# Two Toeplitz convolutions as block-diagonal matrix products between transposes, in place of shifted multiply-adds

## The chip, the cores and the metric

The kernel runs on one core of a Trainium2 chip. The metric is device time in microseconds (us) for one launch. TensorE, VectorE, ScalarE, GpSimd and SyncE are PE, DVE, ACT, POOL and SP in the profile; PEld is PE loading a stationary matrix. Everything is in float32 unless a row says f16.

## What is computed

The input is 8 images of 16 x 16 places with 96 channels, 2048 tokens in all. Four layers follow each other: L0 (a block-wise product in the 2-D Fourier domain, then an MLP), L1 (the Toeplitz layer), and L2 and L3 (each a layer norm, four recurrent GRU passes over 256 steps, a gate and a projection). The change concerns L1:

```python
xn = srms(x)
u = jax.nn.silu(xn @ Wu + bu)
v = jax.nn.silu(xn @ Wv + bv)                # 192 channels
a_h = tno_coeffs(H, r2_...)                  # per channel, 31 lags, from a small network
a_w = tno_coeffs(W, r1_...)
out = tno_apply(v, a_h, -3) + tno_apply(v, a_w, -2)   # by FFT of length 32
return (u * out) @ Wo + bo + x
```

`tno_apply` is, for each channel by itself, a product with a 16 x 16 Toeplitz matrix along the rows (axis 0 in the kernel) or along the columns (axis 1) of the image.

## The kernel before

The order of the work is written out by hand, engine by engine, with semaphores. The program is a row of blocks; all engines meet at the end of each. The ones that matter here are the MLP (function `mlp`) and L1 (function `toeplitz`). All DMAs are issued by SP in the order written.

Two layouts alternate. In a token layout, the 128 partitions are tokens and each of 16 tiles holds 96 channels (`stream`, `rows`). In a channel layout, the partitions are the 96 channels of one of two chunks `m`, and the free dimension is the 2048 tokens, worked in 4 banks of 512 (`xT`, `u`, `v`, `acc`).

The MLP block starts with a norm (`norm_vector`: small chained operations, then 16 row scalings), 16 transposes, and two matrix products. POOL adds a bias to the residual meanwhile.

`toeplitz` does this:
1. Norm and 16 transposes (L139, L163); ACT copies the result into `xT` (L733). POOL adds the output bias to `stream` (L653).
2. 16 products with 512 columns (L766) give `v`, then `u`, in channel layout; ACT applies SiLU twice for `v` (float32 and float16) and once for `u`. POOL makes small diagonal matrices out of the coefficients (L670).
3. The lags. `PE_LAGS` names 18 of the 62 (axis, lag) pairs, done on PE for both chunks as products with float16 diagonal matrices in three parts, accumulated in PSUM (L785). The other 44 pairs are in `DVE_LAGS`: one multiply-add over the shifted image for each chunk, 88 in all, each into the same accumulator `acc` (L692).
4. After the last lag DVE adds PE's part (L714) and multiplies by `u` (L719), 8 times each; PE projects (L798) once the `gated` semaphore allows, bank by bank; DVE adds to `base` (L723) and takes the statistics for the next norm (L147).

Beside this, weights of L2 and L3 are split in a high and a low part: the high part on ACT (L842, L843), the low part on POOL after its diagonals (L848, L851).

The coefficients themselves (`coef`, 96 x 2 x 2 x 31) are ready before the MLP block begins.

## Time and profile before

| | us |
|---|---|
| median of three runs (lowest, highest) | 1206.0 (1205.65, 1208.2) |
| the profiled execution | 1204.91 |
| its span | 1203.1 |
| PE busy in the span | 1085.8 |
| DVE busy | 950.9 |
| ACT busy | 773.5 |
| POOL busy | 154.9 |
| MLP block, by the timeline | 91.2 to 127.5 |
| L1 block | 127.9 to 272.5 |
| L2 from | 272.6 |

The span is the profiler's first to last instruction. It lies 1.8 us below the profiled execution's own time. The two recurrent layers take over 900 us of it. Busy shares are means over the span and say little of one stage; the stage has to be read by windows of time.

### The profile page before, as it was taken

Reading aid. Unit: us, or ns where it says so; the run is one execution under the profiler, and the core shown is the slowest. Engines: PE = TensorE matmul, PEld = TensorE weight load, DVE = VectorE, ACT = ScalarE, POOL = GpSimd, SP = SyncE. Lnnn points to the kernel's source line nnn. Section 1 sums busy time; section 2 is a strip of 40 time slices with the busy share of each in tenths; the row PEclk is TensorE's granted clock in tenths of the full one; section 3 lists DMA queues with packets and bytes.
Section 4 is the critical chain, followed back from the end, with each engine's and each line's share of the span. In section 5 each row is a group of like instructions: output and inputs, shape, how many; then the busy total and the mean of one; then the engine's idle time right before and its main releaser. Section 6 shows DMA issues by size and latency. Waiting matters only on the chain. (4 is left out here: it accounts for less than half of the span.)

```text
span 1203.1 us, 55551 instructions
## 1 busy us (share of the span) xinstructions
PE 1085.8 (90%) x22424; PEld 860.0 (71%) x22424; DVE 950.9 (79%) x5703; ACT 773.5 (64%) x4503; POOL 154.9 (13%) x222
## 2 busy tenths in 40 slices
PE   3787799958999999999999989999999999999997
PEld 2554344445888888888888866788888888888886
DVE  3544699987888888888888876788888888888884
ACT  4223530007788788777777773788788777777773
POOL 1001379920000000001000100000000001000100
PEclk9587899957555555555555556555555555555555
DMA  4000500000000000000000000000000000000000
GB/s 121 2 1 12 133 1 1 1 0 7 4 4 4 4 4 4 4 4 4 4 4 4 3 4 5 4 4 3 4 4 4 4 3 4 4 4 4 4 4 27
DMA packets 8220, 12.59 MB, mean 10 GB/s; under 512 B 5746, under 2 KB 7122, under 8 KB 7675
## 3 DMA queue, kind: packets, MB, share of 16 engines
q1 hardware_dynamic: 7962, 9.05, 3.0%
q8 instruction: 175, 2.87, 1.0%
q14 instruction: 83, 0.67, 0.2%
HBM read 8.26 MB, written 0.79 MB: 8 GB/s over the span
## 5 line engine op out<-in xcount | busy, mean ns | idle before, releaser
L1077 DVE TENSOR_TENSOR_SCAN L3s_h_hi<-L3s_renew,L3s_terms 96x32 f16<-96x32 f32 x512 | 114.5, 224 | 64.3
L1077 DVE TENSOR_TENSOR_SCAN L2s_h_hi<-L2s_renew,L2s_terms 96x32 f16<-96x32 f32 x512 | 114.5, 224 | 64.2
L1185 PE MATMUL L3s_reset_sum<-L3s_h_hi,L_w_hidden 97*128 97x8 f16 x2048 | 139.6, 179 | 11.6 <-DVEq L1054 0.4
L1185 PE MATMUL L2s_reset_sum<-L2s_h_hi,L_w_hidden 97*128 97x8 f16 x2048 | 139.6, 179 | 11.6 <-DVEq L1054 0.4
L1112 POOL TENSOR_TENSOR L_y<-L_states 96x64 f32<-96x64 f32 x128 | 40.9, 355 | 843.1 <-DVE L_states L1079 843.1
L1185 PEld LDWEIGHTS L3s_reset_sum<-L3s_h_hi,L_w_hidden 97*128 97x128 f16 x2048 | 94.4, 107 | 62.1 <-DVE L3s_h_hi L1077 13.8
L1185 PEld LDWEIGHTS L2s_reset_sum<-L2s_h_hi,L_w_hidden 97*128 97x128 f16 x2048 | 94.4, 107 | 62.1 <-DVE L2s_h_hi L1077 13.8
L1133 ACT ACTIVATE L3s_terms<-L3s_cand 96x16 f32<-96x16 f32 x512 | 111.5, 218 | 37.5 <-DVE L3s_cand L1063 6.0
L1133 ACT ACTIVATE L2s_terms<-L2s_cand 96x16 f32<-96x16 f32 x512 | 111.5, 218 | 37.4 <-DVE L2s_cand L1063 5.9
L1185 PE MATMUL L3s_cand_sum<-L3s_h_hi,L_w_hidden 97*128 97x8 f16 x2048 | 131.3, 175 | 4.5 <-DVE L3s_h_hi L1077 3.1
L1185 PE MATMUL L2s_cand_sum<-L2s_h_hi,L_w_hidden 97*128 97x8 f16 x2048 | 131.3, 175 | 4.5 <-DVE L2s_h_hi L1077 3.1
L1185 PE MATMUL L3s_keep_sum<-L3s_h_hi,L_w_hidden 97*128 97x8 f16 x2048 | 130.0, 174 | 0.0
L1185 PE MATMUL L2s_keep_sum<-L2s_h_hi,L_w_hidden 97*128 97x8 f16 x2048 | 130.0, 174 | 0.0
L1128 ACT ACTIVATE L3s_reset<-L3s_reset_sum 96x16 f32<-96x16 f32 x512 | 93.0, 182 | 53.2 <-PE L3s_reset_sum L1185 1.1
L1128 ACT ACTIVATE L2s_reset<-L2s_reset_sum 96x16 f32<-96x16 f32 x512 | 93.0, 182 | 53.2 <-PE L2s_reset_sum L1185 1.0
L1185 PE MATMUL L3s_reset_sum<-L3s_h_lo,L_w_hidden 96*128 96x8 f16 x1024 | 114.1, 185 | 0.5 <-DVE L3s_h_lo L1085 0.2
L1185 PE MATMUL L2s_reset_sum<-L2s_h_lo,L_w_hidden 96*128 96x8 f16 x1024 | 114.0, 185 | 0.4 <-DVE L2s_h_lo L1085 0.2
L1185 PE MATMUL L3s_keep_sum<-L3s_h_lo,L_w_hidden 96*128 96x8 f16 x1024 | 112.1, 183 | 0.0
L1185 PE MATMUL L2s_keep_sum<-L2s_h_lo,L_w_hidden 96*128 96x8 f16 x1024 | 112.1, 183 | 0.0
L1063 DVE TENSOR_TENSOR_SCAN L3s_cand<-L3s_reset,L3s_cand_sum 96x32 f32<-96x32 f32 x512 | 110.4, 216 | 2.0 <-ACT L3s_reset L1128 1.1
L1063 DVE TENSOR_TENSOR_SCAN L2s_cand<-L2s_reset,L2s_cand_sum 96x32 f32<-96x32 f32 x512 | 110.4, 216 | 2.0 <-ACT L2s_reset L1128 1.1
L692 DVE SCALAR_TENSOR_TENSOR l_acc<-l_v,coef,l_acc 96x384 f32<-96x384 f32 (+11 forms) x88 | 103.6, 1241 | 0.4
(257 smaller groups left out, 3517.9 us busy)
## 6 DMA issues: line engine op xcount, KB each, us to landing
L_wih_raw<-in_L_wih SPq DMA_DIRECT2D x2, 1152.0 KB, 11.4
l_w_raw<-in_L_w SPq DMA_DIRECT2D x1, 1296.0 KB
L_w_hidden_raw<-in_L_whh SPq DMA_DIRECT2D x2, 576.0 KB
stream<-in_x SPq DMA_DIRECT2D x2, 384.0 KB, 3.8
out<-stream SPq DMA_DIRECT2D x4, 192.0 KB, 2.1
l_idft<-in_idft SPq DMA_DIRECT2D x1, 400.0 KB
rpe_lw<-in_rpe_lw SPq DMA_DIRECT2D x1, 384.0 KB
l_dft<-in_dft SPq DMA_DIRECT2D x1, 288.0 KB, 2.9
```

What stands on the lines that cost most here:

```text
L692: e.scalar_tensor_tensor(out=row(to, acc), in0=row(of, v), scalar=coef[:, m, axis, at:at + 1], in1=row(to, acc), op0=ALU.mult, op1=ALU.add ...
L1063: e.tensor_tensor_scan(flat(cand[g][:, x]), flat(reset[g][:, x]), flat(cand_sum(g, p)[0:C, :, :, s]), 0.0, ALU.mult, ALU.add).then_inc(can ...
L1077: e.tensor_tensor_scan(flat(h_hi[g][0:C, x]), flat(renew[g][:, x]), flat(terms[g][:, x]), 0.0, ALU.mult, ALU.add).then_inc(hi_ready[g], 1)
L1112: e.tensor_tensor(y[:, m, :, t:t + STEPS].rearrange("p b t -> p t b"), hist[g0][:, t:t + STEPS, j0, :], mirrored, ALU.add)
L1128: e.activation(reset[g][:, x, :, 1], reset_sum(g, p)[0:C, :, s], ACT.Sigmoid).then_inc(advanced[g], 1)
L1133: e.activation(terms[g][:, x, :, 0], cand[g][:, x, :, 1], ACT.Tanh).then_inc(advanced[g], 1)
L1185: return e.matmul(dst, weights.hidden[0:rows, wp, GATES * (2 * g + j) + gate, :], rhs, start=False, stop=False, skip_group_check=True)
```

## The change

The lags disappear from DVE and PE. In their place, for each axis, PE multiplies with matrices of 128 x 128. The 128 entries are 8 channels by 16 places, so that a Toeplitz product is one block-diagonal matrix: `lagged`, for 2 axes and 24 octets of channels.

To fill `lagged`, POOL sets it to zero at the start of the MLP block (128 x 6144 values); SP writes `coef` to a DRAM buffer, waits for that and for the zeros, and issues 16 DMAs of 16 partitions x 24 x 16 values. Each run of 16 values is 64 bytes.

`v` is now made in token layout, once for each axis: 16 tiles of 128 tokens that share one place (row or column), 192 channels each, two to a bank. ACT writes them with one place in every sixteenth element. The bias is a 97th row of `xT` that POOL sets to one. `xT` is stored by row, then image, then column. Then for axis 1 and after it axis 0:
- PE transposes 24 blocks of 128 x 128 (L783) and DVE copies them, four to a copy (L693);
- PE multiplies each with its matrix (L796) and DVE copies the result back into token layout, writing elements 192 apart (L697).

Back in channel layout, PE transposes 32 blocks for axis 1 (L806), and ACT copies them to `both` with elements 256 apart (L746); then 32 blocks for axis 0 (L815), which DVE adds (L706), and multiplies by `u` (L710). The projection waits for halves of the image rather than for quarters. The bias goes into `stream` in place, once the norm has read it.

The diff, cut to its core:

```diff
+                e.dma_start(coefs.rearrange("(m c) a l -> c m a l", m=CHUNKS), coef[:]).then_inc(coefs_written, 16)
+                e.wait_ge(coefs_written, 16)
+                e.wait_ge(cleared, 1)
+                for octet in range(8):
+                    mine = slice(octet * SIDE, (octet + 1) * SIDE)
+                    for axis in range(2):
+                        e.dma_start(lagged[mine, axis, :, mine], lagged_layout(coefs, octet, axis)).then_inc(lagged_loaded, 16)
...
+                e.memset(lagged[:], 0.0).then_inc(cleared, 1)
...
-PE_LAGS = [(axis, lag) for axis, lags in ((0, range(-5, 5)), (1, range(-4, 4))) for lag in lags]
...
+def lagged_layout(coefs, octet, axis):
+    flat_coefs = coefs.rearrange("c a l -> (c a l)")
+    return bass.AP(flat_coefs.tensor, octet * 2 * LAGS + axis * LAGS, [[1, SIDE], [8 * 2 * LAGS, OCTETS], [1, SIDE]])
...
+        xT = sb("xT", [C + 1, TOKENS])
...
+        values = [sb(f"values{axis}", [P, D1 * SIDE]) for axis in range(2)]
+        by_place = [x[:].rearrange("p (c r) -> p r c", r=SIDE) for x in values]
+        convolved = [x[:].rearrange("p (w c) -> p w c", w=SIDE) for x in values]
+        blocks = sb("blocks", [P, OCTETS, P])
+        rows = blocks[:].rearrange("p n q -> p (n q)")[:, 0:TILES * C].rearrange("p (t c) -> p t c", c=C)
+        both = sb("both", [C, CHUNKS, TOKENS])
...
+                e.memset(xT[C:C + 1, :], 1.0).then_inc(ones_ready, 1)
+                e.wait_ge(ones_ready, 1)
+                e.wait_ge(loaded, 96)
+                e.wait_ge(norm.rows_ready, TILES)
+                e.tensor_tensor(stream[:], stream[:], b_o[:].unsqueeze(1).to_broadcast([P, TILES, C]), ALU.add)\
...
-                    e.scalar_tensor_tensor(out=row(to, acc), in0=row(of, v), scalar=coef[:, m, axis, at:at + 1],
-                                           in1=row(to, acc), op0=ALU.mult, op1=ALU.add).then_inc(acc_step[m], 1)
...
+                for a, axis in enumerate(ORDER):
+                    for i in range(GROUPS_OF_4):
+                        e.wait_ge(block_done, GROUPS_OF_4 * a + i + 1)
+                        e.tensor_copy(blocks[:, 4 * i:4 * i + 4, :],
+                                      bank(BLOCKS_AT[a] + i)[:].rearrange("p (n q) -> p n q", n=4)).then_inc(block_saved, 1)
+                    for i in range(GROUPS_OF_4):
+                        e.wait_ge(conv_done, GROUPS_OF_4 * a + i + 1)
+                        e.tensor_copy(convolved[axis][:, :, 32 * i:32 * i + 32].rearrange("p w c -> p c w"),
+                                      bank(CONV_AT[a] + i)[:].rearrange("p (c w) -> p c w", w=SIDE)).then_inc(conv_saved, 1)
...
+                        n = CHUNKS * k + m
+                        mine = both[:, m].rearrange("p (b h w) -> p h b w", b=BATCH, h=SIDE)[:, 4 * k:4 * k + 4]
+                        by_row = lambda x: x.rearrange("p (h b w) -> p h b w", h=4, b=BATCH)
+                        e.wait_ge(first_saved, CHUNKS * NB)
+                        e.wait_ge(back_done, CHUNKS * NB + n + 1)
+                        e.tensor_tensor(mine, mine, by_row(bank(BACK + 8 + n)[0:C, :]), ALU.add)\
+                            .then_inc(both_added, 1)
+                        e.wait_ge(both_added, n + 1)
+                        e.wait_ge(u_ready, CHUNKS * NB)
+                        e.tensor_tensor(mine, mine, by_row(u[:, m, k * BANK:(k + 1) * BANK]), ALU.mult).then_inc(gated, 1)
...
+                    e.activation(by_row[:, 2 * k:2 * k + 2], bank(TURNED + k)[0:C, :].rearrange("p (b h w) -> p b h w", b=2, h=SIDE),
+                                 ACT.Copy).then_inc(copied, 1)
+                for a, axis in enumerate(ORDER):
+                    for i in range(V_GROUPS):
+                        n = V_GROUPS * a + i
+                        e.wait_ge(v_done, n + 1)
+                        e.activation(by_place[axis][:, SIDE - 2 - 2 * i:SIDE - 2 * i, :],
+                                     bank(VALUES + n)[:, 0:2 * D1].rearrange("p (r c) -> p r c", r=2), ACT.Silu).then_inc(v_ready, 1)
...
+                        e.wait_ge(back_done, NB * m + k + 1)
+                        e.activation(both[:, m].rearrange("p (b h w) -> p w h b", b=BATCH, h=SIDE)[:, 4 * k:4 * k + 4],
+                                     bank(BACK + NB * m + k)[0:C, :].rearrange("p (w h b) -> p w h b", w=4, h=SIDE), ACT.Copy)\
+                            .then_inc(first_saved, 1)
...
+                        for slot in range(2):
+                            place = 2 * i + 1 - slot
+                            tile = xT[:, place * P:(place + 1) * P] if axis == 0 else image[:, :, place]
+                            last = e.matmul(bank(VALUES + n)[:, slot * D1:(slot + 1) * D1], tile, w_v[:], start=True, stop=True)
...
+                        for j in range(4):
+                            octet = 4 * i + j
+                            last = e.transpose(bank(BLOCKS_AT[a] + i)[:, j * P:(j + 1) * P],
+                                               values[axis][:, octet * P:(octet + 1) * P], ident[:])
+                        last.then_inc(block_done, 1)
+                    if a == 0:
+                        e.wait_ge(lagged_loaded, 16 * 16)
+                    for i in range(GROUPS_OF_4):
+                        if i < 2 and a == 0:
+                            e.wait_ge(u_ready, 6 + i + 1)
+                        elif i < 2:
+                            e.wait_ge(conv_saved, 4 + i + 1)
+                        e.wait_ge(block_saved, GROUPS_OF_4 * a + i + 1)
+                        for j in range(4):
+                            octet = 4 * i + j
+                            last = e.matmul(bank(CONV_AT[a] + i)[:, j * P:(j + 1) * P], blocks[:, octet, :],
+                                            lagged[:, axis, octet, :], start=True, stop=True)
+                        last.then_inc(conv_done, 1)
...
+                            last = e.transpose(bank(BACK + n)[0:C, j * P:(j + 1) * P],
+                                               convolved[ORDER[0]][:, 4 * k + j, m * C:(m + 1) * C], ident[:])
...
+                        e.wait_ge(first_saved, n + 1)
+                        for j in range(4):
+                            last = e.transpose(bank(BACK + 8 + n)[0:C, j * P:(j + 1) * P],
+                                               convolved[ORDER[1]][:, 4 * k + j, m * C:(m + 1) * C], ident[:])
+                        last.then_inc(back_done, 1)
...
+                    e.wait_ge(gated, 4 * (half + 1))
```

On PE, from the end of the `u` products on, there stood before:

```order
L785 MATMUL l_bank<-l_v_hi,l_diag 128x512 [waits l1_diag_ready,l1_u_ready,l1_v_hi_ready]
L785 MATMUL l_bank<-l_v_hi,l_diag 128x512 x3
L785 MATMUL l_bank<-l_v_hi,l_diag 128x512 [waits l1_diag_ready]
L785 MATMUL l_bank<-l_v_hi,l_diag 128x512 x3
L785 MATMUL l_bank<-l_v_lo,l_diag 128x512 [waits l1_v_lo_ready,l1_diag_ready]
L785 MATMUL l_bank<-l_v_lo,l_diag 128x512 x3
L785 MATMUL l_bank<-l_v_hi,l_diag 128x2x176 [waits l1_diag_ready]
L785 MATMUL l_bank<-l_v_hi,l_diag 128x2x176 x3
```

and this went on for 432 instructions. `l_v_hi`, `l_v_lo` are the float16 parts of `v`, `l_diag` the diagonal matrices. Now there stand, at the end of the first axis's transposes and at the start of the transposes back:

```order
L783 MATMUL l_bank<-ident,l_values 128x128 [waits l1_u_ready]
L783 MATMUL l_bank<-ident,l_values 128x128 x3
L796 MATMUL l_bank<-lagged,l_blocks 128x128 [waits l1_block_saved,l1_u_ready,lagged_loaded]
L796 MATMUL l_bank<-lagged,l_blocks 128x128 x3
L796 MATMUL l_bank<-lagged,l_blocks 128x128 [waits l1_block_saved,l1_u_ready]
L796 MATMUL l_bank<-lagged,l_blocks 128x128 x3
L796 MATMUL l_bank<-lagged,l_blocks 128x128 [waits l1_block_saved]
...
L806 MATMUL l_bank<-ident,l_values 96x128 [waits l1_conv_saved]
L806 MATMUL l_bank<-ident,l_values 96x128 x23
L806 MATMUL l_bank<-ident,l_values 96x128 [waits l1_conv_saved]
```

`l_values` holds SiLU of `v` and later the convolved values, `l_blocks` the transposed blocks. Of the 432 products 48 of another kind are left, and 48 transposes before and 64 behind them are new. The first product waits for `lagged_loaded`.

On DVE, from the norm's row scalings on, there stood before:

```order
L139 TENSOR_SCALAR l_rows<-stream,l1n_rstd 128x96 [waits l1n_chained]
L139 TENSOR_SCALAR l_rows<-stream,l1n_rstd 128x96 x15
L696 MEMSET l_acc 96x2048 x2
L680 TENSOR_TENSOR l_v_lo<-l_v,l_v_hi 96x2048 [waits l1_v_hi_ready]
L692 SCALAR_TENSOR_TENSOR l_acc<-l_v,coef,l_acc 96x8x176 [waits l1_acc_step0]
L692 SCALAR_TENSOR_TENSOR l_acc<-l_v,coef,l_acc 96x8x160 [waits l1_acc_step0] x2
L692 SCALAR_TENSOR_TENSOR l_acc<-l_v,coef,l_acc 96x8x144 [waits l1_acc_step0] x2
```

followed by the rest of the 88 multiply-adds. Now the program has:

```order
L139 TENSOR_SCALAR l_blocks<-stream,l1n_rstd 128x96 [waits l1n_chained]
L139 TENSOR_SCALAR l_blocks<-stream,l1n_rstd 128x96 x15
L693 COPY l_blocks<-l_bank 128x512 [waits l1_block_done] x6
L697 COPY l_values<-l_bank 128x32x16 [waits l1_conv_done] x6
L693 COPY l_blocks<-l_bank 128x512 [waits l1_block_done] x6
L697 COPY l_values<-l_bank 128x32x16 [waits l1_conv_done] x6
L706 TENSOR_TENSOR l_both<-l_both,l_bank 96x4x8x16 [waits l1_back_done,l1_first_saved]
L710 TENSOR_TENSOR l_both<-l_both,l_u 96x4x8x16 [waits l1_u_ready,l1_both_added]
```

and the last two rows seven times more. The 88 dependent multiply-adds, two clears and two subtractions are gone; 24 copies out of PSUM stand in their place, and the additions and products with `u`, eight each as before, now alternate.

## Rows read from the trace of the kernel before

**Rows 1.** Which stages there are: PE, PEld, DVE, ACT, POOL busy, granted clock, DMA.
```profile
91.20:127.50 36.30, 28.27 (x136) 18.91 (x136) 14.24 (x58) 13.05 (x19) 3.42 (x1) 0.77 0.04 10
127.90:155.90 28.00, 19.94 (x48) 6.97 (x48) 22.14 (x47) 19.62 (x33) 9.36 (x12) 0.82 0.61 143
155.90:242.40 86.50, 83.31 (x432) 41.33 (x432) 86.47 (x74) 5.78 (x4) 83.36 (x66) 1.00 0.00 1
242.40:257.00 14.60, 0.03 (x1) 0.03 (x1) 14.29 (x17) 0.00 (x0) 6.63 (x2) 0.57 0.00 0
257.00:272.50 15.50, 13.95 (x64) 13.70 (x64) 12.11 (x32) 0.00 (x0) 0.00 (x0) 0.50 0.00 0
```

**Rows 2.** Groups by line, 140 to 400 us: count, busy, mean ns, idle.
```profile
L692 DVE SCALAR_TENSOR_TENSOR l_acc<-l_v,coef,l_acc 96x384 f32<-96x384 f32 (+11 forms) x88 | 103.6, 1241 | 0.4
```

**Rows 3.** Timeline from 92 us: start, length, engine, line, operation, count, idle.
```profile
92.43 0.17 DVE L122 TENSOR_SCALAR mlpn_power<-mlpn_moments 128x16 f32<-128x16 f32 x1
...
93.80 7.10 DVE L136 TENSOR_SCALAR l_rows<-l_spatial,mlpn_moments,mlpn_rstd 128x96 f32<-128x96 f32 x16
...
94.78 3.42 POOL L417 TENSOR_TENSOR l_residual<-l_residual,mlp_b 128x1536 f32<-128x1536 f32 x1 [35.36 <-DMA mlp_affine<-in_L_norm]
...
120.78 5.50 PE L467 MATMUL l_bank<-mlp_w,mlp_hidden 128*128 128x96 f32 x48
...
130.76 6.55 DVE L139 TENSOR_SCALAR l_rows<-stream,l1n_rstd 128x96 f32<-128x96 f32 x16
...
131.09 3.42 POOL L653 TENSOR_TENSOR l_base<-stream,l_b_o 128x1536 f32<-128x1536 f32 x1 [32.90 <-DMA l_b_o<-in_L_b_o]
...
138.81 16.34 PE L766 MATMUL l_bank<-l_xT,l_w_uv 96*96 96x512 f32 x32 [0.77 <-ACT l_xT L733]
```

**Rows 4.** Timeline around the end of the stage.
```profile
254.44 1.28 DVE L714 TENSOR_TENSOR l_acc<-l_acc,l_bank 96x512 f32<-96x512 f32 x2
...
256.98 13.97 PE L798 MATMUL l_bank<-l_w_o,l_v 96*128 96x96 f32 x64 [14.61 <-DVE l_v L719]
...
270.98 0.56 DVE L723 TENSOR_TENSOR stream<-l_base,l_bank 128x384 f32<-128x384 f32 x1 [2.09 <-PE l_bank L798]
...
275.61 3.92 DVE L136 TENSOR_SCALAR L2i_rows<-stream,L2n_moments,L2n_rstd 128x96 f32<-128x96 f32 x16
```

**Rows 5.** Groups by shape, 235 to 249 us, VectorE.
```profile
L692 DVE SCALAR_TENSOR_TENSOR l_acc<-l_v,coef,l_acc 96x640 f32<-96x640 f32 x2 | 9.8, 4904 | 0.0
L692 DVE SCALAR_TENSOR_TENSOR l_acc<-l_v,coef,l_acc 96x256 f32<-96x256 f32 x1 | 3.3, 3307 | 0.0
```

**Rows 6.** Timeline at the start of the last layer.
```profile
737.40 1.80 POOL L907 MEMSET L_forward<- 1x2048 f16 x1 [20.75 <-POOLq L1234]
...
738.67 0.56 DVE L122 TENSOR_SCALAR L3n_power<-L3n_moments 128x16 f32<-128x16 f32 x1
```

**Rows 7.** Groups by shape, first 127 us: busy, mean ns.
```profile
L389 PE MATMUL l_bank<-l_by_freq,l_idft 100*128 100x384 f32 x32 | 10.9, 497 | 0.9 <-ACT l_by_freq L336 0.9
...
L379 PE MATMUL l_bank<-ident,l_mixed 128*36 128x128 f32 x64 | 8.6, 305 | 1.4 <-ACT l_mixed L328 1.4
...
L318 ACT ACTIVATE l_spectrum<-l_bank,l_affine 96x288 f32<-96x288 f32 x8 | 4.5, 756 | 0.0
...
L247 POOL MEMSET l_by_freq<- 100x3072 f32 x1 | 2.7, 2658 | 3.0 <-POOLq L1297 3.0
...
L300 DVE COPY l_spatial<-l_bank 128x384 f32<-128x384 f32 x4 | 2.2, 558 | 7.5 <-PE l_bank L389 7.5
```

**Rows 8.** The same for 128 to 156 us.
```profile
L733 ACT ACTIVATE l_xT<-l_bank 96x512 f32<-96x512 f32 x4 | 2.4, 594 | 6.5 <-PE l_bank L163 6.5
```

**Rows 9.** Timeline of the first layer's transposes.
```profile
67.21 8.64 PE L379 MATMUL l_bank<-ident,l_mixed 128*36 128x128 f32 x64 [1.35 <-ACT l_mixed L328]
```

**Rows 10.** Granted clock (before the last two) where only transposes run, from 67.2 us.
```profile
66.00:70.00 4.00, 2.79 (x14) 2.01 (x15) 1.47 (x8) 3.31 (x10) 0.00 (x0) 0.50 0.00 0
70.00:72.00 2.00, 2.00 (x19) 1.74 (x18) 1.41 (x5) 1.11 (x4) 0.00 (x0) 0.93 0.00 0
72.00:74.00 2.00, 2.00 (x21) 1.80 (x19) 1.65 (x5) 1.48 (x5) 0.00 (x0) 1.00 0.01 4
```

**Rows 11.** The DMA queue, 127 to 131 us: packets, MB, share of 16 engines.
```profile
q1 hardware_dynamic: 492, 0.35, 41.7%
```

More of the change, by code:

```diff
@@ L390, in _, with mlp @@
                     last.then_inc(inverted, 1)
-def mlp(nc, d, stream, spatial, residual, rows, banks, ident, stats):
+def mlp(nc, d, stream, spatial, residual, rows, banks, ident, stats, coef, coefs, lagged, lagged_loaded):
     with ExitStack() as ctx:
@@ L596, in finish, with toeplitz @@
                         .to_broadcast([C, CHUNKS, 2, LAGS]), ALU.add).then_inc(self.finished, 1)
-PE_LAGS = [(axis, lag) for axis, lags in ((0, range(-5, 5)), (1, range(-4, 4))) for lag in lags]
-PE_LAGS.sort(key=lambda al: al != (0, 0))
-DVE_LAGS = [(axis, lag) for axis in range(2) for lag in sorted(range(1 - SIDE, SIDE), key=abs) if (axis, lag) not in PE_LAGS]
-def shifted(v, axis, lag):
-    n = SIDE - abs(lag)
-    to, of = (slice(lag, SIDE), slice(0, n)) if lag >= 0 else (slice(0, n), slice(-lag, SIDE))
-    return to, of
-def toeplitz(nc, d, stream, ident, coef, weights, stats):
+OCTETS = D1 // 8
+def lagged_layout(coefs, octet, axis):
+    flat_coefs = coefs.rearrange("c a l -> (c a l)")
+    return bass.AP(flat_coefs.tensor, octet * 2 * LAGS + axis * LAGS, [[1, SIDE], [8 * 2 * LAGS, OCTETS], [1, SIDE]])
+def toeplitz(nc, d, stream, ident, lagged, lagged_loaded, weights, stats):
     with ExitStack() as ctx:
@@ L639, in toeplitz, with tiles_of @@
         banks = [ctx.enter_context(nc.psum_tensor(f"l1_bank{i}", [P, BANK], F32)) for i in range(8)]
+        TURNED, VALUES, INNER, BLOCKS_AT, CONV_AT, BACK, OUT = 0, 4, 20, (28, 40), (34, 46), 52, 68
+        bank = lambda n: banks[n % 8]
+        V_GROUPS, GROUPS_OF_4 = SIDE // 2, OCTETS // 4
+        ORDER = (1, 0)
+        def tiles_of(rows, k):
+            first = 8 * (k % 2) + k // 2
+            return rows[:, first:first + 2 * 4 - 1:2, :]
         with nc.Block() as block:
@@ new lines, in _ @@
+                for a, axis in enumerate(ORDER):
[4 more added lines that the diff above has]
+                                     bank(VALUES + n)[:, 0:2 * D1].rearrange("p (r c) -> p r c", r=2), ACT.Silu).then_inc(v_ready, 1)
+                e.wait_ge(loaded, 96)
+                for m in range(CHUNKS):
+                    for k in range(NB):
+                        e.wait_ge(u_done, NB * m + k + 1)
+                        e.activation(u[:, m, k * BANK:(k + 1) * BANK], bank(INNER + NB * m + k)[0:C, :], ACT.Silu,
+                                     bias=b_u[:, m:m + 1]).then_inc(u_ready, 1)
@@ new lines, in _ @@
+                image = xT[:].rearrange("p (n w) -> p n w", w=SIDE)
+                for a, axis in enumerate(ORDER):
+                    for i in range(V_GROUPS):
+                        n = V_GROUPS * a + i
+                        if n >= 8:
+                            e.wait_ge(v_ready, n - 7)
+                        for slot in range(2):
+                            place = 2 * i + 1 - slot
+                            tile = xT[:, place * P:(place + 1) * P] if axis == 0 else image[:, :, place]
+                            last = e.matmul(bank(VALUES + n)[:, slot * D1:(slot + 1) * D1], tile, w_v[:], start=True, stop=True)
+                        last.then_inc(v_done, 1)
@@ new lines, in _ @@
+                e.wait_ge(conv_saved, 2 * GROUPS_OF_4)
+                for k in range(NB):
+                    for m in range(CHUNKS):
+                        n = CHUNKS * k + m
+                        e.wait_ge(first_saved, n + 1)
+                        for j in range(4):
+                            last = e.transpose(bank(BACK + 8 + n)[0:C, j * P:(j + 1) * P],
+                                               convolved[ORDER[1]][:, 4 * k + j, m * C:(m + 1) * C], ident[:])
+                        last.then_inc(back_done, 1)
@@ L792, in _ @@
                 for k in range(NB):
-                    e.wait_ge(gated, CHUNKS * (k + 1))
+                    half = k // 2
+                    e.wait_ge(gated, 4 * (half + 1))
                     for t in range(4):
-                        tile = 4 * k + t
+                        tile = HALVES * (4 * (k % 2) + t) + half
                         for m in range(CHUNKS):
-                            last = e.matmul(banks[k][:, t * C:(t + 1) * C], v[:, m, tile * P:(tile + 1) * P], w_o[:, m, :],
+                            last = e.matmul(bank(OUT + k)[:, t * C:(t + 1) * C], both[:, m, tile * P:(tile + 1) * P], w_o[:, m, :],
```

190 lines of the change are left out of this document (59 added, 131 removed).

## The prediction

> **What bounds the kernel now.** I read the busy time by windows first, because the shares over the whole span are nearly all recurrent layers, which the change does not touch. In the L1 block the reader should see three stretches [rows 1]. From 155.9 to 242.4 us PE, DVE and POOL are all full (83.3, 86.5 and 83.4 of 86.5 us). Then PE stops and DVE goes on alone to about 257. From 257 to 272.5 PE projects at a granted clock of 0.50, that is 1.2 GHz. Second, the groups by line: the 88 lags on DVE are 103.6 us with 0.4 us idle before them [rows 2]. They wait for nothing. Third, the timeline: DVE ends its last lag at 254.44 and the projection starts at 256.98 [rows 4], whereas PE's last lag ends at 242.4. So DVE's chain sets the end, with PE 12 us behind it. Removing DVE's lags alone would be worth 12 us; this change takes both away.
>
> **The sum** is made on the profiled execution (1204.91 us, span 1203.1); the median of the runs, 1206.0, is 1.1 above. Everything before 91.2 and behind 272.5 keeps its length.
>
> (a) *MLP block.* POOL now starts with a clear of 6144 values. One of 3072 took 2.66 [rows 7], so this one takes 5.3, from 91.2 to 96.5. A clear does hold up DVE: in the last layer POOL's ran from 737.40 to 739.20, and the TENSOR_SCALAR that started at 738.67 lasted 0.56 instead of the 0.17 it takes in the MLP [rows 3, 6], to 739.23. In the MLP this same operation starts at 92.43, the row scalings at 93.80 [rows 3]. I let it wait to 96.5. Then POOL's addition of 3.42 follows and, as before (7.10 for scalings that alone take 3.92 [rows 3, 4]), shuts DVE out, to about 100.1. The remaining small operations, then 16 scalings of 3.92, end at 104.5 instead of 100.9: **+3.6**. Bounds 0 (DVE gets in between) and 5.3.
> The DRAM round trip and the 16 DMAs run beside the MLP. They hold 6144 runs of 64 bytes. From 127 to 131 the queue took 41.7% of 16 engines for 492 packets [rows 11]: 0.417 x 16 x 4.0 / 492 = 54 ns each, so 6144 / 16 x 54 ns = 21 us, from about 98 to 119, plus issues. They are needed near 162: 0.
>
> (b) *Norm of L1.* POOL's bias addition (3.42) ran during the row scalings, which took 6.55; it now waits until they are through, and they cost 3.92: **-2.6**. It then runs beside PE and ACT only. The clear of the row of ones is 1.8 long (as the 2048-value clear [rows 6]) and over before the scalings.
>
> (c) *`v` and `u`.* Before: 138.81 to 155.9, 17.1. Now 32 products of 192 columns, two passes each. A warm pass with 384 columns is 10.93/32 = 0.342, one with 96 columns 5.50/48 = 0.115 [rows 3, 7]; these are the bounds, and I take 0.18 for 192: 64 x 0.18 = 11.5. `u` is 16 passes of 512, 0.342 x 512/384 = 0.46 each, 7.3. A slow start is 0.5. Together 19.3: **+2.2**. ACT's 16 SiLUs have 384 values each, written 64 bytes apart. The nearest row writes 288 values 32 bytes apart in 0.56 (4.5/8 [rows 7]), 1.9 ns each, against 0.594/512 = 1.2 for contiguous ones [rows 8]. That gives 0.45 to 0.75 each, 7 to 12 in all, about PE's own time. SP has six loads instead of four to issue ahead of the recurrent weights; they have 10 us until PE needs them.
>
> (d) *From the last `u` to the end of the block.* Before: 155.9 to 272.5, 116.6. Now:
> - Transposes and products, two axes. A transpose is 8.64/64 = 0.135 [rows 7, 9], so 24 are 3.2. A product of 128 columns is two passes of 0.13 (bounds 0.115 and 0.342), 24 are 6.2. Twice 9.4 is 18.8. DVE's 24 copies of 512 values are 0.74 each by the 384-value copy (0.558 [rows 7]), 17.8 in all. Most lie beside PE. The first block copies of an axis must be through before the next products, and so on: four hand-overs of 0.5, 2.0. Sum **20.8**. The writes 768 bytes apart could double half of the copies, which adds about 2.2 for each axis.
> - Back: DVE may add only when ACT has copied all 8 banks of axis 1. ACT takes 0.59 contiguous, 1.0 at the price of the strided row; I take 0.8: 6.4, and 1.0 for the first four transposes and the hand-overs: **7.4**. PE's 64 transposes (8.6) and the second set are hidden behind ACT and DVE.
> - DVE: 16 operations of 0.64 (1.28 for two [rows 4]) and waits of 0.06 are 11.2; the first half of the image is gated at 5.6. PE then projects. Before, it idled 14.6 and then ran all 13.97 at the low clock [rows 1, 4]; now it idles about 5 and I keep the low clock: 7.0 for the first half, to 12.6, 7.0 for the second, to 19.6, and 1.5 for the last addition, statistics and block end: **21.1**. At the high clock it would be 11.2 + 3.8 + 1.5 = 16.5.
> The three make 49.3 instead of 116.6: **-67.3**.
> POOL's low parts of the weights, about 13 us, run from about 164 now, beside DVE's copies. Before, they stretched DVE's lags to 3.3 and 4.9 us [rows 5], but those read two SBUF operands; the copies read PSUM. I take 0; the other end is +10.
>
> Sum: 3.6 - 2.6 + 2.2 - 67.3 = -64.1, which is 1140.8 on the profiled execution and **1142** on the median.
>
> **Two rules weighed.** The clock: in the first layer PE does only transposes from 67.21 to 75.85 [rows 9]. The granted clock is 0.50 up to 70, 0.93 from 70 to 72, then 1.00 [rows 10], so it rose while only transposes ran. The Trainium skill (TensorE: Matmul & The Clock Gate, Part 4: PE-mode transpose) says that transposes don't bring the array to its high clock. By that rule the 24-transpose stretches would drag the clock down; the trace disagrees, but with float32 and 36 columns held, so the case stays a rival; by the rule the sum would be rival 2's 1161, by the trace it is 1142.
> The strides: the only strided ACT row costs 1.6 times a contiguous one per value [rows 7, 8]. The Trainium skill (SBUF — State Buffer, Door 1: The DMA port swizzle) says that SBUF has lines of 16 bytes and that each access crossing to a new line pays. By it all new layouts (64, 768 and 1024 bytes) pay on every value; the trace agrees in direction at 32 bytes. The sum by the rule would be rival 1's.
>
> **The rivals.**
> 1. *Strided accesses cost double* (13%). For: the 1.9 ns row. Against: `v` is only 384 values per operation. Price: 16 SiLUs at 1.5 instead of 0.75 add 12 beyond PE's 11.5, DVE's strided copies 2 x 2.2, ACT's copies back 8 x 0.4: about 19. Time 1161.
> 2. *PE stays at the low clock in (d)* (14%). For: its bursts are short and wait on copies; the projection before ran 14 us busy at 0.50 and did not rise. Against: [rows 10], and `v`, `u` are dense. Price: 18.8 doubled, as all its passes are column-bound: +18.8. Time 1161.
> 3. *Better than the sum* (11%): the clear does not hold DVE (-3.6), the projection runs warm (-4.6), ACT's copies are contiguous-priced (-1.6). Time 1132.
> 4. *POOL blocks DVE's copies too* (5%): +10, 1152.
> 5. *Slower than before* (3%): the 16 loads touch only 16 partitions each. If their runs are spread over few DMA engines, they take 6144 x 54 ns = 332 us on one, from 98 to 430, and the first product, due at about 163, waits 267 us: 1142 + 267 = 1409. It loses from a load that ends 64 us late, at 227, thus below 332/129 = 2.6 engines. Nothing in the trace shows a DMA to 16 partitions. Against it: the 54 ns come from loads of 96 and 128 partitions that kept 41.7% of 16 engines busy.
> That the lags are not really gone is excluded by the order of the instructions.
>
> **How the numbers follow.** The forecast has 54%, with its own range 1133 to 1152. With rivals 1 to 4 the range is 1128 to 1165; outside lie the DMA case, both clock and strides together, and the best cases. A measurement here can tell 0.2%, 2.4 us, from no change. All but rival 5 are faster by far more: faster 0.96, same 0.01, slower 0.03.
>
> **What would show it.** In the changed profile: the MLP's first TENSOR_SCALAR lasting to about 96.5; L1's scalings in 3.9; `v` passes of 0.17 to 0.19 and SiLUs of at most 0.75; 20 us for the transposes and products at a clock of 1.00; ACT's strided copies under 1.0; the projection in two bursts of 7; PE waiting nowhere on `lagged`; L2 starting near 208. It is wrong if PE waits for the loads, if copies out of PSUM last 3 us beside POOL, or if the two recurrent layers change their length.

## The result, and the profile after

The changed kernel takes **1134.96 us** (median of 4 runs, 1133.43 to 1139.38); the kernel before, run beside it, 1205.83 (4 runs). The ratio is **0.9418**, 95% interval 0.9386 to 0.945: faster by 71 us. Run again beside the kernels of experiments 3 and 5, the same kernel took 1137.03 (5 runs, 1133.87 to 1140.01), ratio 0.9444 (0.9423 to 0.9465). Forecast: 1142, range 1128 to 1165.

In the profiled execution (1135.26 us, span 1133.1) the stages stand so:

| stage | before | after | change | forecast |
|---|---|---|---|---|
| up to the MLP block | 91.1 | 92.3 | +1.2 | 0 |
| MLP block | 36.75 | 37.3 | +0.5 | +3.6 |
| L1 to the first `v` product | 10.9 | 7.6 | -3.3 | -2.6 |
| `v` and `u` | 17.2 | 19.2 | +2.1 | +2.2 |
| from the last `u` to L2 | 116.6 | 45.9 | -70.7 | -67.3 |
| L2 to the end | 930.5 | 930.7 | +0.2 | 0 |
| sum | | | -70.0 | -64.1 |

The 1.2 us ahead of the MLP block need not come from the change. In `no_dve_lags` and `one_pe_lag` (experiment 4), which are the kernel before up to L1, this block starts at 92.5 and 92.6 too.

The windows of the changed kernel by stage (length, busy time of PE, PEld, DVE, ACT, POOL with counts, granted clock, DMA share, GB/s) answer to [rows 1]:

```profile
91.20:127.50 36.30, 24.82 (x134) 17.52 (x134) 17.02 (x54) 13.05 (x19) 8.61 (x2) 0.81 0.17 22
129.60:156.50 26.90, 22.92 (x97) 18.03 (x98) 5.25 (x39) 21.89 (x31) 5.24 (x2) 0.87 0.66 149
156.50:173.50 17.00, 16.12 (x146) 15.94 (x144) 16.39 (x23) 6.50 (x5) 12.51 (x4) 1.00 0.00 1
173.50:186.80 13.30, 7.86 (x65) 6.75 (x65) 6.98 (x11) 7.18 (x8) 0.00 (x0) 0.92 0.00 0
186.80:200.80 14.00, 13.95 (x64) 13.71 (x64) 8.88 (x24) 0.00 (x0) 0.00 (x0) 0.50 0.01 1
```

The 86.5 us with three full engines and the 14.6 us of DVE alone are gone. In their place stand 17.0 us in which PE and DVE are both nearly full (16.12 and 16.39 busy), at a granted clock of 1.00; PE sets the pace, for it waits only once. Then follow 13 us in which ACT copies and after it DVE adds, and then the projection, still at 0.50.

The MLP block, as a timeline (start, length, engine, line, operation; idle before and what ended it), answers to [rows 3]:

```profile
92.34 5.22 POOL L425 MEMSET lagged<- 128x6144 f32 x1 [32.27 <-POOLq L233]
93.61 3.98 DVE L122 TENSOR_SCALAR mlpn_power<-mlpn_moments 128x16 f32<-128x16 f32 x1
97.52 3.43 POOL L427 TENSOR_TENSOR l_residual<-l_residual,mlp_b 128x1536 f32<-128x1536 f32 x1
97.65 7.99 SPq L421 DMA_DIRECT2D lagged<-coefs  x16
98.16 2.82 DVE L130 TENSOR_TENSOR mlpn_work<-mlpn_guess 128x16 f32<-128x16 f32 x1
101.43 3.93 DVE L136 TENSOR_SCALAR l_rows<-l_spatial,mlpn_moments,mlpn_rstd 128x96 f32<-128x96 f32 x16
101.82 4.05 PE L163 MATMUL l_bank<-ident,l_rows 128*96 128x128 f32 x16 [13.00 <-DVE l_rows L136]
...
106.73 5.42 PE L468 MATMUL l_bank<-mlp_xT,mlp_w 96*128 96x512 f32 x12 [0.86 <-ACT mlp_xT L447]
```

The reader should compare ends. POOL's clear ends at 97.56 and its addition at 100.95. DVE's operation at 93.61, which took 0.17 before [rows 3], lasts to 97.59; the one at 98.16, 0.17 in `both_late` (experiment 1), lasts to 100.98. Both are held until POOL is through. Not every DVE operation is. The 16 BATCH_NORM_AGGREGATEs at the start (L119) took 1.17 us beside the clear, as they do without it in L1 of the kernel before, and a RECIPROCAL at 97.88 (L129) took its 0.25 beside the addition.

From `v` on:

```profile
132.48 2.96 DVE L139 TENSOR_SCALAR l_blocks<-stream,l1n_rstd 128x96 f32<-128x96 f32 x16
...
137.23 12.53 PE L765 MATMUL l_bank<-l_w_v,l_xT 97*128 97x192 f32 x64 [0.77 <-ACT l_xT L726]
149.60 7.03 PE L771 MATMUL l_bank<-l_xT,l_w_u 96*96 96x512 f32 x16
156.47 2.78 PE L783 MATMUL l_bank<-ident,l_values 128*128 128x128 f32 x24
...
159.09 5.52 PE L796 MATMUL l_bank<-lagged,l_blocks 128*128 128x128 f32 x48
...
173.47 3.70 PE L806 MATMUL l_bank<-ident,l_values 128*96 128x128 f32 x32 [0.88 <-DVE l_values L697]
174.14 7.18 ACT L746 ACTIVATE l_both<-l_bank 96x512 f32<-96x512 f32 x8 [10.90 <-PE l_bank L806]
...
181.36 0.68 DVE L706 TENSOR_TENSOR l_both<-l_both,l_bank 96x512 f32<-96x512 f32 x1 [6.18 <-ACT l_both L746]
...
186.78 13.97 PE L824 MATMUL l_bank<-l_w_o,l_both 96*128 96x96 f32 x64 [4.76 <-DVE l_both L710]
```

PE goes from `v` through `u` (L771), the transposes (L783) and the products (L796) without a gap, twice 24 transposes and 48 passes; its first wait is 0.88 us for DVE's last copy, at 173.47. Then ACT's 8 copies of 0.9 each (L746) hold back DVE's first addition, which idled 6.18. Before the projection PE idles 4.76 (14.61 before [rows 4]).

The groups by line from 155 to 186 us (count, busy, mean ns, idle before):

```profile
L697 DVE COPY l_values<-l_bank 128x512 f32<-128x512 f32 x12 | 11.1, 1113 | 0.0
...
L693 DVE COPY l_blocks<-l_bank 128x512 f32<-128x512 f32 x12 | 7.4, 720 | 21.7 <-PE l_bank L783 21.7
L746 ACT ACTIVATE l_both<-l_bank 96x512 f32<-96x512 f32 x8 | 7.2, 1106 | 10.9 <-PE l_bank L806 10.9
```

### The profile page after: what moved, and what is told of

Its sections match the earlier page's. It is cut to its first block and busy times, and to the rows that moved or that the text cites. A ratio compares the mean times of both kernels' runs of the same rounds, so it can differ in the third digit from the quotient of the medians.

```text
span 1133.1 us, 55089 instructions
## 1 busy us (share of the span) xinstructions
PE 1026.5 (91%) x22248; PEld 850.9 (75%) x22248; DVE 857.8 (76%) x5635; ACT 783.1 (69%) x4511; POOL 78.6 (7%) x149
## 5 line engine op out<-in xcount | busy, mean ns | idle before, releaser
L1211 PEld LDWEIGHTS L3s_cand_sum<-L3s_h_hi,L_w_hidden 97*128 97x128 f16 x2048 | 94.2, 104 | 11.8 <-DVE L3s_h_hi L1103 10.5
L1211 PEld LDWEIGHTS L2s_cand_sum<-L2s_h_hi,L_w_hidden 97*128 97x128 f16 x2048 | 94.2, 104 | 11.6 <-DVE L2s_h_hi L1103 10.3
```

Source lines behind the costliest of these rows:

```text
L1211: return e.matmul(dst, weights.hidden[0:rows, wp, GATES * (2 * g + j) + gate, :], rhs, start=False, stop=False, skip_group_check=True)
```

## The experiments

**1. When is POOL allowed to work? (`clear_late`, `both_late`).** The MLP block grew by 0.5 although the scalings end 3.3 us later after its start. Theory: POOL's two operations hold DVE, and PE's clock gives the loss back. In `clear_late` the clear alone goes behind the scalings, in `both_late` the bias addition as well.

```diff
-                e.memset(lagged[:], 0.0).then_inc(cleared, 1)
                 e.wait_ge(loaded, 80)
+                e.wait_ge(norm.rows_ready, TILES)       # both_late; in clear_late behind the addition
                 e.tensor_tensor(residual[:], residual[:], b2..., ALU.add).then_inc(base, 1)
+                e.memset(lagged[:], 0.0).then_inc(cleared, 1)
```

> The changed kernel, but POOL clears the coefficient matrices only behind the MLP's row scalings (its bias addition stays where it is). Theory 1, the clock gave the time back: DVE's scalings end 3.3 us earlier, but POOL's addition again splits them, PE's 16 transposes come in two groups again, and PE's first MLP products run at the low clock until about 8 us behind them, as in the kernel before. MLP block 36.7 to 37.3 us, total within 1 us of the changed kernel. Theory 2, the clear's hold is a loss of its own: the 12 first MLP products take 5.4 us as in the changed kernel and the block is 3.3 us shorter, 34.0; total 1131.6. Either way the matrices are needed 45 us later and nothing waits for them.

> The changed kernel, but POOL's bias addition and its clear both wait for the MLP's row scalings. Both theories: scalings in 3.9 us unbroken, ending 6.5 us earlier than in the changed kernel (near 98.9), the transposes in one group. Theory 1 (the clock depends on PE's unbroken run): the high clock comes about 4 us behind the first transpose, as in the changed kernel, the 12 first products take 5.4 to 6.5 us and the block shrinks by 5.5 to 6.5 us, to about 31; total 1129. Theory 2 (the clock comes when it comes): products at the low clock to about 107.5, block only 3 us shorter, total 1132.

Measured: `clear_late` 1136.01 us (4 runs, 1132.22 to 1136.79), ratio 0.9422 (0.9398 to 0.9445); `both_late` **1128.14** (1127.73 to 1128.79), ratio 0.9363 (0.9342 to 0.9384). The timeline of `clear_late`:

```profile
95.09 7.17 DVE L136 TENSOR_SCALAR l_rows<-l_spatial,mlpn_moments,mlpn_rstd 128x96 f32<-128x96 f32 x16
96.08 3.48 POOL L426 TENSOR_TENSOR l_residual<-l_residual,mlp_b 128x1536 f32<-128x1536 f32 x1 [36.59 <-DMA mlp_affine<-in_L_norm]
...
102.32 5.22 POOL L429 MEMSET lagged<- 128x6144 f32 x1 [2.77 <-DVE l_rows L136]
103.63 8.78 PE L469 MATMUL l_bank<-mlp_xT,mlp_w 96*128 96x512 f32 x12 [0.87 <-ACT mlp_xT L448]
```

and of `both_late`:

```profile
94.44 3.92 DVE L136 TENSOR_SCALAR l_rows<-l_spatial,mlpn_moments,mlpn_rstd 128x96 f32<-128x96 f32 x16
94.83 4.04 PE L163 MATMUL l_bank<-ident,l_rows 128*96 128x128 f32 x16 [6.55 <-DVE l_rows L136]
98.52 3.42 POOL L427 TENSOR_TENSOR l_residual<-l_residual,mlp_b 128x1536 f32<-128x1536 f32 x1 [39.22 <-DVE l_rows L136]
99.74 5.42 PE L469 MATMUL l_bank<-mlp_xT,mlp_w 96*128 96x512 f32 x12 [0.86 <-ACT mlp_xT L448]
```

In `clear_late` the scalings end at 102.26 (105.36 in the changed kernel), 3.2 us sooner after the block's start. But POOL's addition falls into them, they take 7.17, and the transposes break into 4 and 12. The 12 products behind them then last 8.78 instead of 5.42, 3.4 us more, and the block is as long as before the edit (92.4 to 129.9): theory 1. `both_late` has both: early scalings of 3.92, unbroken transposes, products in 5.42. Its MLP block is 30.8 us (91.8 to 122.6), 6.5 less. This is theory 1 of `both_late` as well. So moving the clear alone gained nothing, and moving both gained 7 of 1135.

Is it the unbroken transposes that raise the clock? In all profiles of this case where they are broken (before, `clear_late`, and experiments 4's two) the 12 products took 8.2 to 8.9 us. Of eight profiles with unbroken ones six show 5.42; but the changed kernel's second profile shows 7.28 and `split_copies` 8.62, after the same instructions:

```profile
101.64 4.04 PE L163 MATMUL l_bank<-ident,l_rows 128*96 128x128 f32 x16 [12.99 <-DVE l_rows L136]
...
106.55 8.62 PE L468 MATMUL l_bank<-mlp_xT,mlp_w 96*128 96x512 f32 x12 [0.87 <-ACT mlp_xT L447]
```

The granted clock is still 0.50 up to 111 us in the first of these two and up to 113 in the second. So all four rows of broken transposes, and two of eight unbroken ones, were followed by a late rise: the gap seems to make it likelier, and does not alone decide it. What else does stays open. These up to 3.2 us are part of the spread between the runs.

**2. The projection's clock and the copies back (`keep_warm`, `split_copies`).** `keep_warm` gives PE five products that nobody reads, behind the last transposes back. `split_copies` gives every other copy back from ACT to DVE, which idled 6.2.

```diff
+                e.wait_ge(both_added, 1)
+                for _ in range(5):
+                    e.matmul(bank(OUT)[:], lagged[:, 0, 0, :], lagged[:, 0, 0:4, :], start=True, stop=True)
                 for k in range(NB):
                     half = k // 2
```

```diff
-                    for k in range(NB):
+                    for k in range(0, NB, 2):                      # ACT
...
+                    for k in range(1, NB, 2):                      # DVE, ahead of its additions
+                        e.wait_ge(back_done, NB * m + k + 1)
+                        e.tensor_copy(both..., bank(BACK + NB * m + k)...).then_inc(saved_too, 1)
```

> The changed kernel with five more products of 512 columns on PE between the last transposes back and the projection, in the time in which PE waits for DVE. Theory 1, the low clock of the projection comes from PE's idle 4.8 us: granted clock stays 1.00, the projection takes 2 x 3.8 us in place of 13.97, the end is set by DVE's last product with u plus 3.8 and 1.4, block end 5 us earlier, total 1130. Theory 2, these products of 96 columns run at the low clock anyway, or the clock falls for another reason: 0 us, or a loss of up to 0.5.

> The changed kernel with the eight copies of axis 1 into channel layout shared: four on ACT, four on DVE, which is idle for 6.2 us there. Theory 1, ACT's 7.2 us of copies is what DVE's additions wait for: the wait shrinks to the larger of 4 x 0.9 and 4 x 0.95 plus the start, block end 2.3 to 3.3 us earlier, total about 1132. Theory 2, PE's 64 transposes back (8.0 us busy) set the pace behind the copies: gain below 1 us.

Measured: `keep_warm` 1133.04 (1130.17 to 1135.25), ratio 0.9402 (0.9375 to 0.9429). In its profile the ten filler passes and the projection:

```profile
181.03 4.56 PE L820 MATMUL l_bank<-lagged 128*128 128x512 f32 x10
185.71 3.81 PE L827 MATMUL l_bank<-l_w_o,l_both 96*128 96x96 f32 x32
190.99 5.08 PE L827 MATMUL l_bank<-l_w_o,l_both 96*128 96x96 f32 x32 [1.47 <-DVE l_both L710]
```

The two halves take 3.81 and 5.08 us, not 7.0 each, and from the first addition to L2 it is 17.4 us (180.29 to 197.69) instead of 21.0 (181.36 to 202.36): 3.6 less. It is less than the clock promises, because the second half waits 1.47 us for DVE, and the granted clock falls during it (1.00 up to 193 us, 0.50 from 194). Theory 1 holds for the first half and only in part for the second. Its total of 1130 came in the profiled execution (1130.17) and not in the median, and the interval overlaps that of the changed kernel, so that the gain is read from the stage alone.

`split_copies` took 1134.1 (1131.14 to 1135.03), ratio 0.9408 (0.9385 to 0.943). From the first transpose back to the first addition it needs 5.2 us (178.57 to 183.76) instead of 7.9, as reckoned; in this execution the low clock in the MLP (above) and at the start of `v` (14.61 instead of 12.53) took back more than that. Theory 1 holds for the wait; in the total alone the gain can't be told from the spread.

**3. Strides (`even_weights`, `even_writes`).** What do the layouts with 64, 768 and 1024 bytes between elements cost, and where is it felt?

```diff
-                            tile = xT[:, place * P:(place + 1) * P] if axis == 0 else image[:, :, place]
+                            tile = xT[:, place * P:(place + 1) * P]                    # even_weights
```

```diff
-                        e.activation(by_place[axis][:, SIDE - 2 - 2 * i:SIDE - 2 * i, :],          # even_writes, 3 places
+                        e.activation(values[axis][:, 2 * D1 * i:2 * D1 * (i + 1)]...,
-                        e.tensor_copy(convolved[axis][:, :, 32 * i:32 * i + 32].rearrange("p w c -> p c w"),
+                        e.tensor_copy(values[axis][:, BANK * i:BANK * (i + 1)]...,
-                            e.activation(both[:, m].rearrange("p (b h w) -> p w h b", ...)[:, 4 * k:4 * k + 4],
+                            e.activation(both[:, m, k * BANK:(k + 1) * BANK]...,
```

> Axis 1's v is made from contiguous tiles of xT, as axis 0's, instead of from columns 64 bytes apart; this leaves out the right order of the columns of axis 1, so its values stand in other places. The strided stationary loads were 0.31 us on average against 0.20 for contiguous ones. Theory 1: ScalarE's SiLUs (0.76 each, 12.2 for 16) pace the stage and PE has slack: v takes 12.5 as before, the program 0 to 0.5 us less, 1134.5 to 1135. Theory 2: PE's strided loads pace the first half: PE's passes of axis 1 fall from 0.22 to 0.17 and v takes 11.0, the program 1133.5.

> ScalarE's SiLUs of v, its copies back, and VectorE's copies of the products write their results one behind another instead of 64, 1024 and 768 bytes apart; the values then stand in the wrong places, this part of the computation is left out. Theory 1 (strides cost, but only where the engine is the bound): the SiLUs fall from 0.76 to about 0.5 each, and v is paced by PE, 12.5 to 11.5; the copies back fall from 0.90 to 0.62 each, 8 of them, 2.2 less; VectorE's copies fall from 0.92 to 0.62 and this is hidden behind PE. Together 2.5 to 3.5 less, 1131 to 1132.5. Theory 2 (the strides cost nothing, the operations are that long by their count): nothing changes, 1135. Theory 3 (VectorE's copies pace the products): 12 x 0.3 = 3.6 more, 1128.

Measured: `even_weights` 1131.91 (1131.04 to 1138.72), ratio 0.941 (0.9384 to 0.9437); `even_writes` 1130.19 (1126.8 to 1135.11), ratio 0.9395 (0.9364 to 0.9426). Both intervals overlap that of the changed kernel, so the operations decide. The changed kernel's `v` is the 12.53 us row above. The groups from 137 to 160 us, first of the changed kernel:

```profile
L765 PEld LDWEIGHTS l_bank<-l_w_v,l_xT 97*128 97x128 f32 x64 | 12.3, 252 | 1.2 <-issue 1.2
L733 ACT ACTIVATE l_values<-l_bank 128x384 f32<-128x384 f32 x16 | 11.8, 828 | 0.5
```

of `even_weights`:

```profile
L765 PE MATMUL l_bank<-l_w_v,l_xT 97*128 97x192 f32 x64 | 10.6, 327 | 0.8 <-ACT l_xT L726 0.8
L765 PEld LDWEIGHTS l_bank<-l_w_v,l_xT 97*128 97x128 f32 x63 | 10.3, 190 | 0.0
L733 ACT ACTIVATE l_values<-l_bank 128x384 f32<-128x384 f32 x16 | 10.6, 850 | 0.0
```

of `even_writes`, with its copies from 155 to 186 us:

```profile
L733 ACT ACTIVATE l_values<-l_bank 128x384 f32<-128x384 f32 x16 | 7.9, 491 | 4.0 <-PE l_bank L765 4.0
```

```profile
L697 DVE COPY l_values<-l_bank 128x512 f32<-128x512 f32 x12 | 8.0, 686 | 1.1 <-PE l_bank L796 1.0
...
L746 ACT ACTIVATE l_both<-l_bank 96x512 f32<-96x512 f32 x8 | 4.0, 609 | 9.8 <-PE l_bank L806 9.8
```

The strided stationary loads cost 1.9 us: with contiguous tiles `v` takes 10.6 instead of 12.5, at a granted clock of 1.00 in both, and now ACT's SiLUs fill the time without a gap. So theory 2 of `even_weights` holds, with 10.6 for its 11.0, and theory 1, that ACT paced `v`, fails. ACT's strided writes cost 828 against 491 ns, and nothing is won when they alone go, since `v` still takes 12.5 at the pace of PE's loads. That part of theory 1 of `even_writes` (11.5) fails; its part on the copies back holds. The copies back are 1106 against 609 ns, and there it shows: 8 of them in 4.0 us instead of 7.2. DVE's copies are 1113 against 686 ns and hide behind PE but for the wait of 0.88 at the end: the 17.0 us from the first transpose to the transposes back become 16.0. From the start of `u` to DVE's first addition it is 27.5 us (148.91 to 176.40) instead of 31.8. A strided write is thus 1.6 to 1.8 times a contiguous one on either engine, and cost the stages from `u` to the addition 4.3 us here, 3.2 of them at the copies back. Beside that, PE then idled 2.94 instead of 4.76 ahead of the projection, which took 12.43 instead of 13.97.

**4. Was DVE the bound, and how far behind was PE? (`no_dve_lags`, `one_pe_lag`, edits of the kernel before).**

```diff
-DVE_LAGS = [... if (axis, lag) not in PE_LAGS]
+DVE_LAGS = [... if False]                # no_dve_lags
+PE_LAGS = PE_LAGS[:1]                    # one_pe_lag, after DVE_LAGS is made
```

> The kernel before, with VectorE's 88 multiply-adds left out (their 44 pairs of axis and lag are missing from the result), TensorE's 18 pairs, with GpSimd's diagonals, kept. Theory 1: VectorE's chain was the bound and TensorE stood 12 us behind it. TensorE's last lag ended at 242.4, fed by GpSimd's diagonals (83 of 86.5 us busy); without VectorE it ends at about 240, then 8 additions and products and the projection: the end of L1 comes 12 to 15 us earlier, 1189 to 1192. Theory 2: VectorE's lags slow GpSimd (VectorE's lags near the end took 3.3 and 4.9 us beside it) and GpSimd's diagonals speed up much without them: the end comes 25 us or more earlier, under 1180. Theory 3: TensorE or GpSimd were the bound: 1204.

> The kernel before, with only one of TensorE's 18 pairs of axis and lag kept, and all of VectorE's 88 multiply-adds (17 pairs are missing from the result). Theory 1: VectorE's chain is the bound; it runs from 141 to 254 with no idle time whatever TensorE does. Without GpSimd's 400 small diagonals VectorE's lags that were stretched near the end (3.3 and 4.9 us) get back to about 1.2, 3 to 5 us: 1199 to 1202. Theory 2: the 83 us of GpSimd's diagonals slow all of VectorE's lags: 10 us or more, under 1194. Theory 3: TensorE set the end: 1190 or less.

Measured beside each other: before 1205.53 (7 runs); `no_dve_lags` 1192.72 (1188.98 to 1194.34), ratio 0.9886 (0.9864 to 0.9908); `one_pe_lag` 1197.53 (1192.96 to 1198.64), ratio 0.9918 (0.9892 to 0.9943). Taking away 104 us of work on DVE was worth 13 us, taking away nearly all of PE's lags 8. `no_dve_lags` came 0.7 us above the range of its theory 1; `one_pe_lag` lies between the ranges of theories 1 and 2, so POOL's diagonals cost DVE more than the few stretched lags that theory 1 counted. The groups of `no_dve_lags` from 140 to 256 us:

```profile
L670 POOL TENSOR_SCALAR l_diag<-ident,l_coef_parts 96x128 f16<-96x128 f32 x69 | 40.8, 601 | 51.8 <-PE l_bank L785 51.8
```

the same row of the kernel before:

```profile
L670 POOL TENSOR_SCALAR l_diag<-ident,l_coef_parts 96x128 f16<-96x128 f32 x66 | 78.0, 1199 | 18.1 <-PE l_bank L785 18.1
```

and of `one_pe_lag`:

```profile
L693 DVE SCALAR_TENSOR_TENSOR l_acc<-l_v,coef,l_acc 96x384 f32<-96x384 f32 (+11 forms) x88 | 94.8, 1140 | 0.4
```

The reader should see the means. POOL's diagonals take 601 ns each without DVE beside them, 1199 with it. DVE's 88 lags take 94.8 us without POOL's diagonals, 103.6 with them [rows 2]. That is 8.8 us, and L1 became 8.0 us shorter. `one_pe_lag` takes PE's products away together with the diagonals, but POOL alone can do this: from 244 to 249 us in the kernel before PE did nothing, and a lag of 256 values took 3307 ns beside POOL [rows 5], whereas two of this size took 482 each after POOL's end at 249.2.

Was POOL, then, the next bound behind DVE? No. In `no_dve_lags` POOL waits 51.8 us for PE, and PE's own products still last 81.9 us (158.63 to 240.54) where they had lasted 86.4 (155.97 to 242.36). PE was the next bound, 13 us behind DVE. Only a change that relieves DVE and PE both gets at the rest of the 71 us.

**5. Together (`combined`).** `both_late`, `keep_warm` and `split_copies` in one kernel.

> The clear and the bias addition behind the norm's row scalings (6.9 us of 1135 when done alone), ten filler passes on PE ahead of the projection (about 5 in its own profile: the projection's first 32 passes in 3.8 instead of 7.0, and the second 32 too), and half of the copies back given to VectorE (2.7: 5.19 instead of 7.89 us from the first transpose back to the first addition). Theory 1: the three lie one behind the other on the critical path and add, 1135 - 14.6 = 1120.5, range 1118 to 1124. Theory 2: the filler collides with the copies or the last transposes back once VectorE copies too, and its gain is lost: 1125 to 1128.

> The changed kernel once more, beside the other three. Theory 1: whether the granted clock rises to 1.00 before or within the first 12 products of the MLP differs from run to run: these last 5.4 or about 8.6 us after the same 16 transposes, and the time lies at 1133 or 1136 accordingly, median 1134 to 1136. Theory 2: the unbroken row of transposes fixes the rise: 5.42 always, and the spread comes from elsewhere.

Measured: `combined` **1121.75** us (6 runs, 1119.85 to 1129.37), ratio 0.9332 (0.9304 to 0.9359); the changed kernel beside it 1137.03. In its profile:

```profile
177.16 3.71 PE L836 MATMUL l_bank<-l_w_o,l_both 96*128 96x96 f32 x32
181.77 5.94 PE L836 MATMUL l_bank<-l_w_o,l_both 96*128 96x96 f32 x32 [0.90 <-DVE l_both L719]
```

MLP block 30.7 (37.3), first transpose back to first addition 5.2 (7.9), first addition to L2 18.3 (21.0): 12.0 us of the 15.2 by which the span is shorter; 0.9 lie ahead of the MLP and 2.2 in the recurrent layers, which the edits don't touch. The gains add, except that the second half of the projection runs 5.94 as the clock falls; theory 1. Two of the six executions took 1129.2 and 1129.4 us and the other four 1119.9 to 1122.0; the trace is of one of the four, and what the two lost stays open. This is the fastest version here.

For the changed kernel itself theory 2 is out, since its 12 products took 7.28 us this time and not 5.42. Theory 1 had expected either 5.4 or 8.6 and a median of 1134 to 1136; it was 1137.03.

## Why the prediction was right, point by point

The likeliest case came in, 7 us below its forecast and inside its own range. The mechanism was right: the stage from the last `u` to L2 gave -70.7 where -67.3 was forecast, and all other stages together +0.7. Some smaller terms were right only because errors cancelled, as said below. Step by step:

- *(a) MLP, +3.6: the mechanism right, the sum wrong.* The clear took 5.22 and held DVE as said, scalings 3.3 later. What I left out is that the addition, behind the clear, now falls ahead of the row scalings and no longer into them. That left the scalings and PE's transposes unbroken, and the clock was high when the products began. The windows, with the granted clock before the last two numbers:

```profile
100.00:104.00 4.00, 2.18 (x10) 1.43 (x10) 3.90 (x14) 0.79 (x2) 0.95 (x1) 0.50 0.56 48
104.00:106.00 2.00, 1.87 (x8) 1.06 (x7) 1.37 (x6) 1.63 (x3) 0.00 (x0) 0.50 0.51 49
106.00:107.00 1.00, 0.27 (x1) 0.27 (x2) 0.00 (x0) 0.98 (x2) 0.00 (x0) 0.91 0.49 45
107.00:108.00 1.00, 1.00 (x3) 0.41 (x3) 0.00 (x0) 0.99 (x2) 0.00 (x0) 1.00 0.00 0
```

  PE worked only 0.27 us of the stretch from 106 to 107, whose mean is 0.91, so the clock rose before the first product at 106.73, when PE had done 16 transposes and nothing else since it had idled 13.00 us. The 12 products took 5.42 instead of 8.17, which gave 2.75 back. A term for "PE later" has to ask at what clock PE then runs. Experiment 1 shows that this holds in most executions, not in all.
- *(b) -2.6, measured -3.3.* The scalings took 2.96 instead of 6.55. I had priced them at the MLP's 3.92, but that form does two operations with two scalar operands per partition and this one does one with one; which of the two differences counts isn't shown. Of the 3.6 us won, 0.3 was lost again, since PE's transposes, at the low clock, took 3.65 and now ended 1.0 us behind the scalings (0.7 before).
- *(c) +2.2, measured +2.1.* This was luck. From the first product to the first transpose it was 19.2 us for 19.3, but `v` took 12.4 (11.5 in the sum), `u` 6.9 (7.3), and the slow start of 0.5, a term from no row, did not come: the granted clock was 1.00 from the start. I had priced all passes of `v` alike at 0.18, while those of axis 1 paid for strided loads, mean 313 ns up to 143.3 us, against 207 for those of axis 0:

```profile
L765 PEld LDWEIGHTS l_bank<-l_w_v,l_xT 97*128 97x128 f32 x28 | 6.2, 313 | 1.2 <-issue 1.2
```

```profile
L765 PEld LDWEIGHTS l_bank<-l_w_v,l_xT 97*128 97x128 f32 x37 | 6.3, 207 | 0.0
```

- *(d) -67.3, measured -70.7.* The largest miss is in the transposes and products, 17.0 for 20.8: a transpose and a product pass were both 0.115 to 0.116, the lower bound, where I had taken 0.135 and 0.13. The four hand-overs of 0.5 came from no row; PE waited once, 0.88 us, as DVE's block copies (0.62 apart) kept pace. Back 7.9 for 7.4, at 0.90 a copy for 0.8. DVE and the projection 21.0 for 21.1.
- *Rival 1 (strides double), out:* strided writes cost 1.6 to 1.8 times, near the 1.6 of the one strided row of before, but most lay beside other work. The Trainium skill (SBUF — State Buffer, Door 1: The DMA port swizzle) says that each access that crosses to a new 16-byte line pays. The trace agrees in direction (828 against 491 ns for values 64 bytes apart), and the page gives no factor.
- *Rival 2 (low clock), out.* A window of the first transposes and products:

```profile
156.00:160.00 4.00, 4.00 (x35) 3.67 (x34) 2.90 (x5) 3.80 (x4) 1.14 (x1) 1.00 0.00 0
```

  It stood at 1.00 through both sets of transposes, and also from 173.5 to 184, where PE did transposes only, up to 182.0. The Trainium skill (TensorE: Matmul & The Clock Gate, Part 4: PE-mode transpose) says that transposes don't bring the high clock. The trace disagrees a second time, in the MLP, where the clock rose after 13.00 us of idle PE and 16 transposes (windows under (a)).
- *Rival 3 (everything better), not as described:* its three gains (no held DVE, a warm projection, cheaper copies back) all stayed out. The time lies below the forecast by the transposes, the hand-overs and the MLP's clock.
- *Rival 4 (POOL blocks the copies), out.* POOL's low parts ran from 158.9 to 171.7, and the copies beside them came 0.62 and 0.92 apart; the block copies before POOL began were 0.62 apart too. POOL held two DVE operations in the MLP that read and write SBUF, and none here, where DVE reads PSUM. That the PSUM operand is the reason isn't varied by itself.
- *Rival 5 (DMAs to 16 partitions), out.* The queue from 95 to 125 us:

```profile
q1 hardware_dynamic: 6743, 0.45, 15.8%
```

  The last DMA is issued at 105.6, and the median one lands 2.0 us behind its issue. A packet took 0.158 x 16 x 30 / 6743 = 11 ns, not 54; 6144 of these packets are the runs of 64 bytes. My 54 came from packets of some 700 bytes (0.35 MB in 492 [rows 11]).
